# W11's pieces laid out one by one, a new order of the first unit's work, two rows' statistics on VectorE, and three aggregations joined

## The reference

```
g   = sigmoid(xn @ gate_w.T + gate_b);  u_g = xn * g
y   = c * (G * cumsum over time of (b * u_g / G)) + d_eff * u_g     # d_eff from the mean of u_g
p   = softmax(xn @ wr.T)                      # 8 experts, the best 2, gates normalized
h   = silu(xn @ w1.T); h = silu(h @ w3.T); h = h @ w2.T
out = zeros_like(xn); out[expert index] += gate * h      # rows 0 to 7 only
x   = x + y * silu(out)
```

## Time and profile before

| | |
|---|---|
| median of three runs | 766.77 us |
| the profiled execution | 767.88 us, span 766.1 us |
| mean granted TensorE clock | 0.995 |
| instructions | 8776 |
| HBM read, written | 95.60 MB, 37.77 MB |

### The profile page before, as it was taken

How to read it: one execution, slowest core, us unless ns; L and a number is a source line. 1 busy time by engine, 2 the same in 40 slices (tenths; PEclk the granted TensorE clock), 3 DMA queues, 4 the chain that set the end, 5 groups by cost and what they waited for, 6 DMA issues and landing times.

```text
span 766.1 us, 8776 instructions
## 1 busy us (share of the span) xinstructions
PE 753.8 (98%) x3568; PEld 598.8 (78%) x3568; DVE 505.8 (66%) x471; ACT 347.8 (45%) x451; POOL 40.4 (5%) x52
## 2 busy tenths in 40 slices
PE   6999999999999999999999999999999999999997
PEld 6868877887778777888788878778777778777875
DVE  6789789674967576469998997565524553456321
ACT  5769965835663426233843372225223331333121
POOL 3300103020300100000000000000000000000000
PEclk8999999999999999999999999999999999999999
DMA  9743674536543534465596713222230423110500
GB/s 329 284 166 138 234 236 176 191 139 199 175 136 123 179 110 165 158 242 210 213 346 213 278 70 133 114 110 82 110 138 6 187 83 117 48 56 1 221 1 3
DMA packets 27400, 117.20 MB, mean 153 GB/s; under 512 B 3440, under 2 KB 3680, under 8 KB 20320
## 3 DMA queue, kind: packets, MB, share of 16 engines
q1 hardware_dynamic: 18112, 99.85, 35.9%
q10 hardware_dynamic: 9248, 16.80, 5.9%
HBM read 95.60 MB, written 37.77 MB: 174 GB/s over the span
## 4 chain that ended last, share of the span: by engine, by line
PE 91%; DVE 4%; ACT 2%; DMA 1%; issue 1%; SPq 0%; DVEq 0%
PE main L1002 29%; PE main L1003 28%; PE main L1004 28%; PE lgp L1068 2%; PE spare L1095 1%; PE lgp L1095 1%; DMA wl2f<-wB 1%; DVE x3r L1147 1%; PE main L1130 0%; PE lgp L1075 0%; DVE bc L1147 0%; DVE x3f L1147 0%; DVE x5r L1147 0%; DVE x8f L1147 0%; DVE wl6f L1147 0%
## 5 line engine op out<-in xcount | busy, mean ns | idle before, releaser
L1147 DVE TENSOR_TENSOR s<-s,main 128x512 f32<-128x512 f32 x72 | 48.6, 682 | 64.8 <-PE main L1004 64.6
L1147 DVE TENSOR_TENSOR u<-u,main 128x512 f32<-128x512 f32 x36 | 24.5, 685 | 45.7 <-PE main L1004 45.7
L932 ACT ACTIVATE u<-u 128x512 f32<-128x512 f32 x32 | 20.0, 631 | 56.6 <-DVE u L1147 56.6
L1147 DVE TENSOR_TENSOR u<-s,main 128x512 f32<-128x512 f32 x32 | 21.6, 684 | 34.2 <-PE main L1004 34.2
L932 ACT ACTIVATE s<-s 128x512 f32<-128x512 f32 x32 | 20.0, 630 | 52.5 <-DVE s L1147 52.5
L913 ACT ACTIVATE s<-main 128x512 f32<-128x512 f32 x36 | 20.8, 594 | 48.1 <-PE main L1004 22.1
L932 ACT ACTIVATE rows<-rows 128x512 f32<-128x512 f32 x16 | 10.1, 632 | 71.3 <-DVE rows L1147 71.3
L1147 DVE TENSOR_TENSOR rows<-s,main 128x512 f32<-128x512 f32 x16 | 11.0, 686 | 30.4 <-PE main L1004 30.4
L932 ACT ACTIVATE u<-main 128x512 f32<-128x512 f32 x32 | 18.8, 593 | 20.7 <-PE main L1004 20.5
L862 ACT ACTIVATE rows<-rows,nm 128x1024 f32<-128x1024 f32 x24 | 27.7, 1153 | 0.8
L860 ACT ACTIVATE rows<-rows 128x1024 f32<-128x1024 f32 x25 | 26.1, 1046 | 1.9 <-DMA rows<-x 1.8
(11 more groups left out here) (696 smaller groups left out, 2432.1 us busy)
## 6 DMA issues: line engine op xcount, KB each, us to landing
out<-x SPq DMA_DIRECT2D x31, 512.0 KB, 7.5
rows<-x SPq DMA_DIRECT2D x26, 512.0 KB, 4.2
H_d<-u ACTq DMA_DIRECT2D x32, 256.0 KB, 4.3
H_d<-s ACTq DMA_DIRECT2D x16, 256.0 KB, 3.1
rows<-xh_d SPq DMA_DIRECT2D x16, 256.0 KB, 5.0
w2f<-w2T SPq DMA_DIRECT2D x2, 2048.0 KB, 10.7
wl6f<-wB SPq DMA_DIRECT2D x3, 1024.0 KB, 8.5
wl4f<-wB SPq DMA_DIRECT2D x3, 1024.0 KB, 6.0
```

Of the source, the lines that this page charges most:

```text
L932: ins = eng.activation(dst, src, ACT.Silu)
L1147: return eng.tensor_tensor(o, a, b, op)
```

## The change

There are four edits. (1) W11's four pieces come from an array of their own, `w11`, in which each piece is one stretch of 256 KB; before, a piece was every fourth 2 KB of the block. (2) The list of unit 0's steps has a new order: row 2 is loaded ahead of pieces 2 and 3; the tile copies stand ahead of pieces 2 and 3 on ScalarE; a second `WARM` of 12 transposes goes to the bank `main[0]`; tiles 4 and 5 are copied, transposed and subtracted in product 1 and no longer between the parts of product 0; the routing products come ahead of product 3 and no longer inside it. (3) The statistics of rows 11 and 15 go to VectorE (bn_stats); their means and deviations come to `mvu` by two small POOL steps, and the three steps that follow row 11 stand one tile earlier. (4) In units 5 to 7 the aggregations of products 4, 5 and 6 all stand behind the second tile of the next unit; before, each stood behind the second tile of the product that follows.

```diff
+BN_ROWS = (11, 15)
@@ plan
-            at(0, 1, 0, "TR", 6)
-            at(0, 1, 0, "LZ", 0)
-            at(0, 1, 0, "TE", 6, 0)
-            at(0, 1, 0, "TE", 6, 1)
-            at(0, 1, 0, "LZ", 1)
-            at(0, 1, 0, "NB", 7)
-            at(0, 1, 0, "TD", 2)
-            at(0, 1, 0, "HQ", 2)
-            at(0, 1, 0, "WO", 0, 3)
-            at(0, 1, 1, "TR", 7)
...
+            for step in (("TR", 4), ("TE", 4, 0), ("TE", 4, 1), ("TR", 5), ("TE", 5, 0), ("TE", 5, 1), ("TD", 0), ("HQ", 0),
+                         ("S", 0, 3), ("WH", 0, 3), ("TD", 1), ("HQ", 1), ("LZ", 0), ("NB", 7), ("LZ", 1)):
+                at(0, 1, 0, *step)
+            for step in (("TR", 6), ("TE", 6, 0), ("TE", 6, 1), ("TD", 2), ("HQ", 2), ("WO", 0, 3)):
+                at(0, 1, 1, *step)
+            for step in (("TR", 7), ("TE", 7, 0), ("TE", 7, 1), ("LZ", 2), ("TD", 3), ("HQ", 3), ("LZ", 3)):
+                at(0, 1, 2, *step)
...
+            for b in "acbd":
+                at(0, 1, 3, "LQ", 0, b)
...
-            for b in "acbd":
-                at(0, 2, 1, "LQ", 0, b)
...
-                    at(m, *divmod(k + 2, 4), "MVC", 2 * n + t // 4)
-                    at(m, *divmod(k + 5, 4), "MV", 2 * n + t // 4)
-                    at(m, *divmod(k + 5, 4), "BC", 2 * n + t // 4)
+                    c, v = (1, 4) if r == 11 else (2, 5)
+                    at(m, *divmod(k + c, 4), "MVC", 2 * n + t // 4)
+                    at(m, *divmod(k + v, 4), "MV", 2 * n + t // 4)
+                    at(m, *divmod(k + v, 4), "BC", 2 * n + t // 4)
@@ the list of unit 0
-    steps = [("WARM", 0), ("ROW", 0), ("ROW", 1)] + [("W0", k) for k in range(4)] + [("ROW", 2), ("ROW", 3), ("WL", 0, 6, "12"),
+    steps = [("WARM", 0), ("ROW", 0), ("ROW", 1), ("W0", 0), ("W0", 1), ("ROW", 2), ("W0", 2), ("W0", 3), ("ROW", 3), ("WL", 0, 6, "12"),
              ("ROW", 4), ("ROW", 5), ("ROW", 6), ("ROW", 7), ("WL", 0, 5, "21"), ("WL", 0, 4, "22"), ("CST", 0),
-             ("NA", 0), ("NA", 1), ("NB", 0), ("TR", 0), ("NB", 1), ("TR", 1),
-             ("WH0", 0), ("WH0", 1), ("WH0", 2), ("WH0", 3), ("TE", 0, 0), ("WO0", 0), ("TL", 0, 0), ("NA", 2), ("TE", 1, 0), ("TL", 1, 0),
-             ("TE", 0, 1), ("TE", 1, 1), ("WO0", 1), ("WO0", 2), ("NA", 3), ("NB", 2), ("WO0", 3),
-             ("MP", 0, 0), ("MP", 0, 1), ("TR", 2), ("MP", 0, 2), ("MP", 0, 3), ("NA", 5), ("NB", 3), ("TR", 3),
-             ("NS", 4), ("TE", 2, 0), ("TE", 2, 1), ("NA", 6), ("TL", 2, 0), ("TE", 3, 0), ("TL", 3, 0), ("TE", 3, 1),
-             ("MP", 1, 0), ("MP", 1, 1), ("NB", 4), ("TR", 4), ("MP", 1, 2), ("MP", 1, 3), ("WH", 0, 1),
-             ("XS", "a"), ("XS", "c"), ("TL", 0, 1), ("TL", 1, 1), ("TL", 2, 1), ("TL", 3, 1), ("NB", 5), ("TR", 5), ("WO", 0, 1),
-             ("TE", 4, 0), ("TE", 4, 1), ("NS", 7), ("PO", 0, 0, 0), ("PO", 0, 0, 1), ("PO", 0, 0, 2), ("PO", 0, 0, 3),
-             ("TE", 5, 0), ("TE", 5, 1), ("NB", 6), ("TD", 0), ("HQ", 0), ("S", 0, 3), ("WH", 0, 3), ("TD", 1), ("HQ", 1), ("ROW", 8), ("ROW", 9)]
+             ("NA", 0), ("NA", 1), ("NB", 0), ("TR", 0), ("NB", 1), ("TR", 1), ("WARM", 1),
+             ("WH0", 0), ("WH0", 1), ("TE", 0, 0), ("TE", 1, 0), ("WO0", 0), ("NA", 2), ("TL", 0, 0), ("TL", 1, 0), ("MP", 0, 0),
+             ("WH0", 2), ("WO0", 1), ("MP", 0, 1), ("WH0", 3), ("TE", 0, 1), ("TE", 1, 1), ("NA", 3), ("NB", 2),
+             ("WO0", 2), ("MP", 0, 2), ("NB", 3), ("TR", 2), ("TR", 3), ("WO0", 3), ("MP", 0, 3), ("WH", 0, 1),
+             ("TE", 2, 0), ("TL", 2, 0), ("TE", 3, 0), ("TL", 3, 0), ("TE", 2, 1), ("TE", 3, 1), ("NS", 4),
+             ("MP", 1, 0), ("MP", 1, 1), ("MP", 1, 2), ("MP", 1, 3), ("XS", "a"), ("XS", "c"),
+             ("TL", 0, 1), ("TL", 1, 1), ("TL", 2, 1), ("TL", 3, 1), ("WO", 0, 1), ("NA", 5), ("NB", 4), ("NA", 6),
+             ("PO", 0, 0, 0), ("PO", 0, 0, 1), ("PO", 0, 0, 2), ("PO", 0, 0, 3), ("NB", 5), ("NS", 7), ("NB", 6), ("ROW", 8), ("ROW", 9)]
@@ aggregations
             if before[0] >= L2 and before[1] in OUT_OF:
-                steps.append(("PH", *before))
+                if before[1] == 6:
+                    steps.extend(("PH", before[0], q) for q in (4, 5, 6))
+                elif before[1] == 1 or before[0] == NN - 1:
+                    steps.append(("PH", *before))
@@ the rows' statistics
+                        stats_in(wait, last - 1)
+                        link(eng.tensor_scalar(mvu[:, h, 0, 3:4], mv0[:, last % 8, 0:1], 1.0, None, ALU.mult))
+                        link(eng.tensor_scalar(mvu[:, h, 1, 3:4], mv0[:, last % 8, 1:2], EPS, None, ALU.add))
...
+                elif kind == "STAT" and s[1] in BN_ROWS:
+                    r = s[1]
+                    row_loaded(wait, r)
+                    st = bst[:, r // 4 % 2, :]
+                    eng.bn_stats(st[:, 0:6], row_buf(r)[:, 0:HT])
+                    link(eng.bn_stats(st[:, 6:12], row_buf(r)[:, HT:D]))
+                    eng.bn_aggr(mv0[:, r % 8, :], st).then_inc(s_sb, 1)
@@ W11
-                    eng.dma_start(w_f(2, 1)[:, k, :], wB[0, 0, 0, :, k, :]).then_inc(s_w0[k], 16)
+                    eng.dma_start(w_f(2, 1)[:, k, :], w11[k]).then_inc(s_w0[k], 16)
...
+        "w11": np.ascontiguousarray(t["L0_ffn_w1"][:HT, :HT].T.reshape(4, P, HT)),
```

More of the change, by code:

```diff
@@ L363, in places_of, with program @@
     raise ValueError("no place for the last rows")
-def program(nc, x, xT, wB, w2T, small, out):
+def program(nc, x, xT, wB, w11, w2T, small, out):
     steps = plan()
@@ L546, in program @@
         s_st2 = sem("s_st2")
+        s_sb = sem("s_sb")
         s_mv = sem("s_mv")
@@ L586, in row_loaded, with stats_in @@
                 wait(s_row[4 + r % 2], 16 * ((r - 8) // 2 + 2))
+        def stats_in(wait, r):
+            of = [q for q in range(8, r + 1) if (q in BN_ROWS) == (r in BN_ROWS)]
+            wait(s_sb if r in BN_ROWS else s_st2, len(of))
         def sums(t):
@@ L720, in _ @@
                     if r >= 10:
-                        wait(s_st2, r - 9)
+                        stats_in(wait, r - 2)
                     elif r >= 8:
@@ L767, in _ @@
                     if k < 4:
-                        wait(s_st2, 24)
+                        stats_in(wait, 8 * GATE - 2)
+                        stats_in(wait, 8 * GATE - 1)
                     else:
@@ L830, in _ @@
                     h = s[1] % 2
-                    wait(s_st2, 4 * k)
+                    last = 8 + 4 * k - 1
+                    stats_in(wait, last)
                     if k > 2:
                         wait(s_mvt, k - 2)
-                    eng.tensor_scalar(mvu[:, h, 0, :], acs[:, h, 0, :], 1.0 / D, None, ALU.mult)
-                    link(eng.tensor_scalar(mvu[:, h, 1, :], acs[:, h, 1, :], 1.0 / D, EPS, ALU.mult, ALU.add))
+                    if last in BN_ROWS:
+                        stats_in(wait, last - 1)
+                        link(eng.tensor_scalar(mvu[:, h, 0, 3:4], mv0[:, last % 8, 0:1], 1.0, None, ALU.mult))
+                        link(eng.tensor_scalar(mvu[:, h, 1, 3:4], mv0[:, last % 8, 1:2], EPS, None, ALU.add))
+                    m = 3 if last in BN_ROWS else 4
+                    eng.tensor_scalar(mvu[:, h, 0, 0:m], acs[:, h, 0, 0:m], 1.0 / D, None, ALU.mult)
+                    link(eng.tensor_scalar(mvu[:, h, 1, 0:m], acs[:, h, 1, 0:m], 1.0 / D, EPS, ALU.mult, ALU.add))
                     eng.tensor_tensor(mvu[:, h, 1, :], mvu[:, h, 1, :], mhalf[:, :], ALU.pow).then_inc(s_mv, 1)
@@ L945, in _ @@
                     r = s[1]
-                    k, h, t = nth(*s), r // 4 % 2, r % 4
+                    h, t = r // 4 % 2, r % 4
+                    if r in BN_ROWS:
+                        continue
                     row_loaded(wait, r)
@@ L1009, in _ @@
                     wait(s_id, 1)
-                    for q in range(34):
-                        eng.transpose(spare[:, q % 4 * P:(q % 4 + 1) * P], ident[:, :], ident[:, :])
+                    idle = main[0] if s[1] else spare
+                    for q in range(12 if s[1] else 34):
+                        eng.transpose(idle[:, q % 4 * P:(q % 4 + 1) * P], ident[:, :], ident[:, :])
                     wait(s_id, 2)
@@ L1025, in _ @@
                     half, k = s[1:]
-                    wait(s_tel, nth("TL", 2 * half + 1, 0))
+                    wait(s_tel, max(nth("TL", 2 * half + t, 0) for t in range(2)))
                     wait(s_wo0, k + 1)
```

## The result

The changed kernel takes 761.36 us (median of 6 runs, 761.23 to 761.47) against 766.85 before: a ratio of 0.9927, 95% interval 0.9915 to 0.9940. The prediction was 760.3 with a range of 758.0 to 764.3. The span of the profiled execution went from 766.1 to 759.6 us, by 6.5. The forecast for that was 6.1 to 6.8.

What follows compares the result with a forecast made beforehand. TensorE, busy 753.8 of 766.1 us, bounds the kernel. Unit 1's earlier start (-4.6 or -3.9) and joined aggregations (-2.2) give -6.8 or -6.1; -6.5 from the 766.77 median makes 760.3 us, range 758.0 to 764.3.

Steps and rivals of the forecast that it cites:

- The start: Unit 0 up to product 0: VectorE's shorter chain lets the first matmul start at 12.6 to 13.4 us instead of 15.02.
- the lower end: First matmul of product 0 at 12.6 us, if row 2 has landed by 9.8.
- the upper end: First matmul at 13.4 us, if W11's pieces land no sooner than before and row 2 follows 1.25 us behind 9.3.
- The wait ahead of the routing products: Before product 3 in unit 0: TensorE waits 1.0 us for ScalarE's copy of tile 7, bounds 0 and 3.
- What is late next: Product 2 to unit 1: VectorE's leads shrink, a 0.8 us wait comes, unit 1 starts at 103.6, 4.6 us earlier.
- a lead of 5.6 us at product 2: Unit 0: product 2 starts at 57.0 instead of 62.64, 5.6 us ahead of the kernel before.
- rival 4: VectorE stands at row 11's statistics until that row lands late; slower from 6.5 us on; 0.09 with similar waits, half slower.
- The aggregations: Units 5 to 7: joining three aggregations saves 2 x 0.36 us of switches per unit, 2.2 us in all.
- the last of the sum: Whole kernel: -6.8 or -6.1 against the profiled 767.88 us, taken as -6.5 from the median 766.77, giving 760.3.
- the late row 2: Start of unit 0: row 2 lands later, so unit 1 gains 3.9 us instead of 4.6 and the sum is -6.1.
- I take the clock as held: Product 0: with WARM 1 the first 24 matmuls cost 2.96 us, not 5.29, and the next tile's transposes 0.3 less.
- a burden: Before unit 1: statistics of rows 11 and 15 add 2 x 1.44 = 2.9 us to VectorE; unit 1 waits 0.8.

Runs made afterwards that it cites:

- the last experiment: Changed kernel with product 1's first two silus and first store put behind tile 7's copies, and the last unit's aggregations of products 4 and 5 joined: 759.48 us.

## Why the prediction was right

**The start.** 12.6 us was worked out for the first matmul (12.65), 26.6 for product 1 (26.84), 46.0 for product 3 (46.39), 57.0 for product 2 (57.42). VectorE's chain was the one that set it, and the pieces landed early enough for the lower end. The prediction could not know the landing and kept both ends; the run with the old layout (13.41) shows that the upper end, 13.4, belongs to that layout. The wait ahead of the routing products was given as 1.0 and is 1.26; moving the silus shows that it hung on ScalarE's list.

**What is late next.** 103.6 was worked out for unit 1, and it is 103.78. The wait there was taken as 0.8 and is 0.37, with VectorE going into unit 1's normalization at 91.19 (91.2 was worked out). Here two misses cancel, and that is luck: product 2 came 0.4 us later than worked out, and the wait was 0.4 shorter. The working itself goes from a lead of 5.6 us at product 2 to 5.4 at unit 1 without saying where the 0.2 went. Row 11 was there when VectorE came to its statistics (68.81), so the late landing of rival 4 did not come.

**The aggregations.** 2.2 us were predicted; 2.05 and 2.1 us are measured, in both kernels.

**The step that was mis-sized** is the last of the sum, which carried a difference of profiled executions over to the median. The spans fell by 6.5 us, the medians by 5.5. In the profiled execution of before the low level lasted over all 24 first matmuls (5.29 us). The kernel with only the joined aggregations has the same list of steps at the start, and in its profile the 24 matmuls took 20.07 - 15.54 = 4.53 us:

```profile
15.54 0.58 PE L1005 MATMUL main<-x2r,wh0r 128*128 128x256 f32 x1 [4.94 <-DVE x3r L1150]
...
20.07 0.60 PE L1024 MATMUL main<-ident,wh5f 128*128 128x128 f32 x4
```

So before, the time lost to the clock changes from one execution to the next. That the profiled one lost more than the median fits this, but only one execution of the kernel before was profiled, so it is not shown. The prediction named the 1.1 us between profile and median and then left it: 6.5 lies between 6.1 and 6.8. Taken from the profiled execution, the sum gives 767.88 - 6.8 = 761.1 (761.8 with the late row 2), and that execution of the changed kernel took 761.42. The three runs behind the 766.77 were also on the low side: beside the last experiment the kernel before took 767.58 and the changed one 761.34, 6.2 us less, within 6.1 to 6.8.

**Two reasons were wrong, though the sum was not.** First, "I take the clock as held" by `WARM` 1: without the 12 transposes the median is the same, so in three of five executions the earlier first matmul was enough by itself; and in the kernel before the same 12 transposes win nothing that can be told. Neither edit alone held the clock each time; both together did in all eleven executions of the changed kernel (mean granted clock 0.999 to 1.0). Second, the statistics of rows 11 and 15 were booked as a burden, 2.9 us on VectorE and a wait at unit 1. I looked only at the engine that gets the work. The one that gives it away was on the path: with the early start ScalarE ends row 15's statistics beside VectorE's passes, POOL's two small steps take 4.4 us instead of 0.4, TensorE stands at the transposes of the means for 2.21 us, and the edit saves 1.6 us. The burden was small: VectorE comes to its passes at 90.94 without the two rows and at 91.19 with them.

## What to carry to other kernels

When a start is brought forward, ask of every later cross-engine step whether it moves along as far; the one that does not (here the row statistics, 2.6 us against 3.9) can end up beside work that it used to precede, and becomes a stall on the in-order engine that waits for it. A term that hangs on the clock scatters from run to run, so take it from several executions, and fill an idle time with work that has to be done anyway, as the routing products do. A table load or a silu that nobody waits for belongs behind the copies that the next product needs.

## What the runs showed of the hardware that was not expected

Two POOL steps on four columns, 0.23 and 0.19 us ahead of VectorE's long passes, took 2.14 and 2.22 us beside them. Idle times of TensorE in which, or right behind which, the granted clock fell were 4.94, 4.61, 3.93, 3.27 and 2.66 us in the profiled executions; 2.21 (at the transposes of the means), 1.47, 1.40 and 0.79 us left it at 1.00. After a fall in mid-kernel, 512-column matmuls started 0.43 us apart instead of 0.23.
